# FFN products of blocks 2 on by seven quarter products in place of eight

## The reference, cut to what matters

```python
x = x + layernorm(attn(layernorm(x), wq, wk, wv, wo))   # 16 heads of 64, window 256
h = layernorm(x)
real = h @ cos(theta + theta_noise)                     # [.., 1024] @ [1024, 1024]
imag = h @ sin(phi + phi_noise)
x = x + layernorm(sqrt(real * real + imag * imag))
```

## Time and profile before

| | us |
|---|---|
| median of 3 runs | 2647.22 |
| profiled execution | 2645.41 |
| its span (slowest core) | 2643.8 |
| TensorE busy | 2593.6 |
| VectorE busy | 1252.0 |
| ScalarE busy | 890.6 |
| GpSimd busy | 522.3 |

### The profile page before, as it was taken

One profiled execution on the slowest core, in us unless ns is written; L12 is line 12 of the kernel. 1 busy time (PEld: TensorE's weight loads), 2 busy tenths in 40 slices (PEclk: granted clock), 3 DMA queues, 4 the chain that ended last, 5 costly groups with the idle time before them and its releaser, 6 DMA issues.

```text
span 2643.8 us, 46661 instructions; the slowest of 8 cores (2638.6 to 2643.8 us)
## 1 busy us (share of the span) xinstructions
PE 2593.6 (98%) x17088; PEld 1566.2 (59%) x17088; DVE 1252.0 (47%) x2564; ACT 890.6 (34%) x2061; POOL 522.3 (20%) x676
## 2 busy tenths in 40 slices
PE   7899999999999999999999999999999999999998
PEld 6566575757576666657575666667544444444443
DVE  5445454545454544445454444444463444344442
ACT  4334352525252433424232333333252222222221
POOL 0112132222222221222222121212231101011010
PEclk9999999999999999999999999999999999999999
DMA  7101212212212122220102020110513343333431
GB/s 258 65 18 71 57 64 57 73 41 73 53 61 65 49 65 64 77 60 25 41 25 65 1 65 11 54 33 33 168 58 106 85 120 87 113 99 93 120 83 53
DMA packets 173777, 185.68 MB, mean 70 GB/s; under 512 B 131824, under 2 KB 132080, under 8 KB 173040
## 3 DMA queue, kind: packets, MB, share of 16 engines
q1 hardware_dynamic: 173552, 182.69, 23.5%
HBM read 109.25 MB, written 41.94 MB: 57 GB/s over the span
## 4 chain that ended last, share of the span: by engine, by line
PE 91%; DVE 2%; DMA 2%; ACT 2%; issue 2%; SPq 0%; DVEq 0%; POOL 0%; ACTq 0%; POOLq 0%
PE pb L662 25%; PE pb L289 21%; PE pb L364 13%; PE pb L330 13%; PE pb L429 7%; PE pb L506 6%; PE pb L470 5%; PE pb L564 2%; DMA r_sb<-phb 1%; DMA r_sb<-thb 1%; DVE stats L446 1%; DVE pb L444 0%; SPq L59 0%; ACT p_sb L449 0%; DVE o_sb L611 0%
## 5 line engine op out<-in xcount | busy, mean ns | idle before, releaser
L289 PE MATMUL pb<-xth,wreg 128*128 128x256 bf16 x3840 | 694.0, 273 | 0.0
L458 POOL TENSOR_SCALAR p_sb<-p_sb,stats 128x384 f32<-128x384 f32 (+2 forms) x512 | 345.6, 687 | 1286.1 <-DVE stats L454 614.4
L449 ACT ACTIVATE p_sb<-pb,stats 128x384 f32<-128x384 f32 (+2 forms) x512 | 287.4, 562 | 754.7 <-DVE stats L446 725.7
L289 PE MATMUL pb<-xtl,wreg 128*128 128x256 bf16 x1920 | 523.8, 273 | 0.0
L289 PEld LDWEIGHTS pb<-xth,wreg 128*128 128x128 bf16 x3840 | 375.4, 98 | 109.5 <-issue 64.9
L444 DVE TENSOR_TENSOR pb<-pb,mask_s 128x256 f32<-128x256 f32 (+1 forms) x512 | 210.1, 410 | 324.2 <-PE pb L429 324.1
L662 PE MATMUL pb<-wreg,q_sb 128*128 128x512 bf16 x1536 | 333.0, 379 | 0.0
L364 PE MATMUL pb<-wreg,aoh 128*128 128x512 bf16 x1024 | 309.7, 379 | 0.0
L330 PE MATMUL pb<-wreg,xth 128*128 128x512 bf16 x1024 | 306.2, 381 | 2.3 <-DVE v_sb L342 1.4
L662 PE MATMUL pb<-wreg,xth 128*128 128x512 bf16 x1024 | 306.0, 379 | 0.0
L446 DVE TENSOR_REDUCE stats<-pb 128x1 f32<-128x384 f32 (+2 forms) x512 | 272.8, 533 | 54.2 <-DVE pb L444 1.8
(11 more groups left out here) (63 smaller groups left out, 2408.2 us busy)
## 6 DMA issues: line engine op xcount, KB each, us to landing
x_sb<-x SPq DMA_DIRECT2D x64, 512.0 KB, 4.4
r_sb<-x SPq DMA_DIRECT2D x32, 512.0 KB, 4.7
x<-r_sb SPq DMA_DIRECT2D x32, 512.0 KB, 2.6
wreg<-x SPq DMA_DIRECT2D x32, 512.0 KB, 6.8
y<-wreg SPq DMA_DIRECT2D x64, 256.0 KB, 2.3
trig<-o_sb SPq DMA_DIRECT2D x32, 256.0 KB, 2.8
wreg<-trig SPq DMA_DIRECT2D x4, 2048.0 KB, 18.9
wreg<-wkT SPq DMA_DIRECT2D x4, 1024.0 KB, 14.6
```

Of the source, the lines that this page charges most:

```text
L289: e.matmul(bank[b][:, 0:256], a, r, start=s, stop=z)
L449: texp = ac.inc(lambda e, e2=e2, pu=pu, sc=sc: e.activation(pu, sc, AF.Exp, bias=stats[:, col + e2:col + e2 + 1], scale=1.0, accum_out=sta ...
L458: tok["p", e2, qs] = po.inc(lambda e, e2=e2, pu=pu: e.tensor_scalar(pu, pu, stats[:, col + 4 + e2:col + 5 + e2], 1.0, op0=ALU.mult, op1=AL ...
```

## The change

From block 2 on, the product of a block's rows with a matrix is made of seven products of quarters in place of eight (Strassen's scheme in Winograd's form). A is the block's 256 x 1024 rows, cut into 128 x 512 quarters; B the matrix, cut into 512 x 512 quarters. Four sums of quarters of A are made in float32 on VectorE for each block, four of B (T1 to T4) once. Sums and quarters are then split into high and low parts as before. A product is 4 chunks of K x 3 matmuls of 512 columns. Some products go on in a bank that holds an earlier one; such a bank is first copied (`keep`) or totalled with a kept one (`total`).

The sums of B are made with the chunks: a chunk is now 256 columns out of each half of the columns, of the two 128-row chunks kc and kc+4. There are 16 chunks as before, with 11 parts in place of 7; one in each of groups 1 to 14, two in groups 7 and 14, queued at the end of s=1 in place of s=2. The sums go to a new DRAM tensor, 8 MB of high and low parts in all, and are loaded at the end of the attention stage into wreg[3], k_sb and v_sb. All eight banks serve the FFN from block 2 on, LayerNorm parts stay in `later`, and one part of `later` and one of the next rows' is popped after each product.

```diff
-            which, kc = i // KC, i % KC
+            which, kc, c0 = i // 8, i % 8 // 2, i % 2 * 256
             a, b = r_sb[:, 0:1024], r_sb[:, 1024:2048]
-            return [lambda: trig_load(which, kc, a, b), lambda: None, lambda: None,
+            return [lambda: trig_load(which, kc, c0, a, b), lambda: None, lambda: None,
                     lambda: trig_sum(which, a, b), lambda: trig_sin(which, a, b),
-                    lambda: trig_high(b), lambda: trig_low(which, kc, b)]
+                    lambda: (trig_high(b), quarter_sums(a, b, 0)),
+                    lambda: (trig_low(b), trig_store(which, kc, c0), quarter_sums(a, b, 1)),
+                    lambda: quarter_sums(a, b, 2), lambda: None,
+                    lambda: trig_high(a), lambda: (trig_low(a), sums_store(which, kc, c0))]
...
+        def trig_load(which, kc, c0, a, b):
             sp.wait(tok.get("x2"), tok.get("trig_free"), tok.get("wo_stage"))
             for n, dst in enumerate((a, b)):
-                tok["trig_in"] = sp.dma(c_tl, dst, tr_d[which][n][kc * 128:(kc + 1) * 128, :])
+                for i in range(2):
+                    r0 = (kc + 4 * i) * 128
+                    src = tr_d[which][n][r0:r0 + 128, :].rearrange("p (j c) -> p j c", j=2)[:, :, c0:c0 + 256]
+                    tok["trig_in"] = sp.dma(
+                        c_tl, dst[:, i * 512:(i + 1) * 512].rearrange("p (j c) -> p j c", j=2), src)
...
+        def quarter_sums(a, b, n):
+            q = lambda v, i, w=1: v[:, i * 256:(i + w) * 256]
+            dv.wait(tok["trig_sin"], tok.get("quarters"))
...
+        def trig_high(v):
+            ac.wait(tok["trig_sin"], tok.get("quarters"), tok.get("o_free"), tok.get("trig_st"))
+            tok["trig_hi"] = ac.inc(lambda e: e.activation(obf[:, 0:1024], v, AF.Copy))
...
+        def rows_parts(b):
...
+            def sums12():
+                t = diff(s1, a21, a22, ALU.add, st["xn", 1], *tok["s_rows"])
+                st["s", 0] = diff(s2, s1, a11, ALU.subtract, t)
+
+            def sums34():
+                diff(s3, a11, a21, ALU.subtract, st["xn", 0])
+                st["s", 1] = diff(s4, a12, s2, ALU.subtract, st["s", 0])
...
+            def turn_a():
+                sp.wait(tok["wino", b % 2], st["h", "a"], st["l", "a"], st["h", "a2"], st["l", "a2"])
+                for n, (c, w) in enumerate(((0, 1024), (1024, 512))):
+                    for dst, src in ((dah, xnh), (dal, alo)):
+                        tok["aw", n] = sp.turn(
+                            c_xw[n], dst[:, c:c + w].rearrange("p (k t) -> p k t", t=128), src[:, c:c + w])
...
+            return [lambda: stat(0), lambda: stat(1), rstd, lambda: app(0),
+                    lambda: (app(1), high_a()), lambda: (sums12(), high_a2()),
+                    lambda: (sums34(), high_s(0)), lambda: (low_a(), high_s(1)),
+                    lambda: (low_a2(), turn_a()), lambda: (low_s(0), turn_s(0)),
+                    lambda: (low_s(1), turn_s(1), ends())]
...
+            def p6(r):
+                pe.wait(st["p1", r])
+                t = product(r, "a", ("s", 1), ("t", T2))
+                st["u2", r] = keep(r, "a", 2 + r, t)
...
+            return [lambda f=f, r=r: f(r) for f in (p1, p2, p6, p7, p5, p4, p3) for r in range(2)]
...
-                if s == 2 and g > 0:
-                    for i in range((g - 1) * tpp, min(g * tpp, 2 * KC)):
+                if s == 1 and g > 0:
+                    for i in range((g - 1) * 16 // (NB - 2), min(g * 16 // (NB - 2), 16)):
                         later += trig_chunk(i)
...
+        load_sums(0, [tok["o_pe", NB - 1]])
...
+        turn["banks"] = tuple(range(8))
+        for b in range(2, NB):
+            load_resid2(b)
+            rows = rows_parts(b + 1) if b + 1 < NB else []
+            for n, f in enumerate(wino(b)):
+                f()
+                if later:
+                    later.pop(0)()
+                if n > 0:
+                    run(rows, 1)
```

More of the change, by code:

```diff
@@ L92, in build_nc @@
     trig_d = nc.dram_tensor("trig", [2, 2, 128, KC * D], BF16).ap()
+    sums_d = nc.dram_tensor("sums", [2, 2, 128, 8192], BF16).ap()
     with contextlib.ExitStack() as ctx:
@@ L132, in build_nc @@
         c_y = [new(f"d_y{i}") for i in range(2)]
+        c_ws = [new(f"d_ws{i}") for i in range(2)]
+        c_xw = [new(f"d_xw{i}") for i in range(4)]
         tok = {}
@@ L615, in trig_low, with trig_store @@
+        def trig_store(which, kc, c0):
+            sp.wait(tok["trig_hi"], tok["trig_lo"])
             for n in range(2):
-                tok["trig_st"] = sp.dma(c_ts, trig_d[which, n, :, kc * D:(kc + 1) * D],
-                                        obf[:, n * 1024:(n + 1) * 1024])
+                for i in range(2):
+                    o = (kc + 4 * i) * D
+                    dst = trig_d[which, n, :, o:o + D].rearrange("p (j c) -> p j c", j=2)[:, :, c0:c0 + 256]
+                    src = obf[:, n * 1024 + i * 512:n * 1024 + (i + 1) * 512].rearrange("p (j c) -> p j c", j=2)
+                    tok["trig_st"] = sp.dma(c_ts, dst, src)
+            tok["o_free"] = tok["trig_st"]
@@ L618, in trig_low, with sums_store @@
+        def sums_store(which, kc, c0):
+            tok["trig_free"] = tok["trig_lo"]
+            sp.wait(tok["trig_hi"], tok["trig_lo"])
+            for n in range(2):
+                dst = sums_d[which, n].rearrange("p (q k) -> p q k", q=4)[:, :, kc * 512 + c0:kc * 512 + c0 + 256]
+                src = obf[:, n * 1024:(n + 1) * 1024].rearrange("p (q c) -> p q c", q=4)
+                tok["trig_st"] = sp.dma(c_ts, dst, src)
             tok["o_free"] = tok["trig_st"]
@@ L726, in ffn, with load_sums @@
             return out
+        pbf, ptbf, wbf = p_sb[:].bitcast(BF16), pt_sb[:].bitcast(BF16), wreg[3][:]
+        qrt = [((pbf[:, 0:1536], pbf[:, 1536:3072]), (aoh[:], aol[:])),
+               ((ptbf[:, 0:1536], ptbf[:, 1536:3072]), (xth[:], xtl[:]))]
+        sums = [(wbf[:, 0:8192], wbf[:, 8192:16384]), (k_sb[:].bitcast(BF16), v_sb[:].bitcast(BF16))]
+        hold = [q_sb[:, i * 512:(i + 1) * 512] for i in range(4)]
+        T1, T3, T2, T4 = range(4)
+        def load_sums(r, waits):
+            sp.wait(*waits)
+            for n in range(2):
+                tok["ws", r] = sp.dma(c_ws[r], sums[r][n], sums_d[r, n])
@@ new lines, in wino, with product, keep, part @@
+        def wino(b):
+            par = b % 2
+            bk, st = {}, {}
+            def product(r, name, xp, wp):
+                first = (r, name) not in bk
+                if first:
+                    bk[r, name] = dense_bank()
+                    pe.wait(*bfree[bk[r, name]])
+                bank_ = bank[bk[r, name]]
+                kind, p = xp
+                xh, xl = qrt[par][kind == "s"]
+                pe.wait(tok["wx", par, kind, p], tok["wt", r])
+                if wp[0] == "t":
+                    pe.wait(tok["ws", r])
+                t = None
+                for kc in range(4):
+                    c = p * 512 + kc * 128
+                    if wp[0] == "t":
+                        o = wp[1] * 2048 + kc * 512
+                        ws_h, ws_l = (v[:, o:o + 512] for v in sums[r])
+                    else:
+                        ws_h, ws_l = (f(r, kc + 4 * wp[1], wp[2] * 512, 512) for f in (wh, wl))
+                    for i, (a, w) in enumerate(three(xh[:, c:c + 128], xl[:, c:c + 128], ws_h, ws_l)):
+                        f = lambda e, a=a, w=w, s=(first and kc == 0 and i == 0), z=(kc == 3 and i == 2): \
+                            e.matmul(bank_[:], a, w, start=s, stop=z, skip_group_check=not first)
+                        if kc == 3 and i == 2:
+                            t = pe.inc(f)
+                        else:
+                            pe.do(f)
+                return t
+            def keep(r, name, n, t):
+                ac.wait(t, tok.get(("hold", n)))
+                src, dst = bank[bk[r, name]], hold[n]
+                te = ac.inc(lambda e: e.activation(dst, src[:], AF.Copy))
+                st["keep", n] = te
+                return te
+            def part(r, tt, nh):
+                o = tt * 1024 + nh * 512
+                return (sq, mg)[r][:, o:o + 512]
+            def square(r, tt, nh, src, t):
+                dst = part(r, tt, nh)
+                ac.wait(t, tok.get(("mg", tt, nh)))
+                te = ac.inc(lambda e: e.activation(dst, src, AF.Square))
+                if r == 1:
+                    later.extend(ln_m(b, tt, nh, nh != tt, dst, part(0, tt, nh), te))
+                return te
+            def total(r, name, n, tt, nh, t):
+                dst, src = part(r, tt, nh), bank[bk[r, name]]
+                dv.wait(t, st["keep", n], tok.get(("mg", tt, nh)))
+                te = dv.inc(lambda e: e.tensor_tensor(dst, src[:], hold[n], ALU.add))
+                tok["hold", n] = te
+                square(r, tt, nh, dst, te)
+                return te
+            def p1(r):
+                t = product(r, "a", ("a", 0), ("b", 0, 0))
```

(40 more changed lines are left out.)

93 lines of the change are left out of this document (75 added, 18 removed).

## The result

The changed kernel takes 2682.62 us (median), the kernel before 2647.52: ratio 1.0127, 95% interval 1.0096 to 1.0157. It is slower by some 33 us, where 2657, some 10 us, was forecast. Its profiled execution took 2678.75 us. Runs in which a die was disturbed are left out of the ratio, but are part of the medians that are given.

The account below looks back on a forecast made before the run. TensorE was taken to bound both the FFN and attention stages. The terms -72.5 (FFN), +1 (end), -11.5 (old chunks), +82.6 (first-chunk stall) and +10 (second chunks) sum to +9.6 on 2647.2: 2657 us, range 2618 to 2690.

Parts of the forecast that it names:

- FFN, -72.5: FFN blocks: 168 matmuls in place of 192, 5.18 us less in each of 14 blocks, if TensorE stays the bound.
- FFN blocks don't keep TensorE fed: Rival, FFN blocks: transposes or VectorE come 1.5 us late in each, 21 us more, 2678 us; chance 0.10.
- End, +1: Last block: its last LayerNorm stands on VectorE behind the other rows' apply; between 0 and 2.6 us, taken as +1.
- Stall of the first chunk: Attention groups 1 to 14: VectorE waits 5.5 us at the sum for its load, delaying masks, exponential and TensorE; +82.6 us.
- I take +6.2: First chunk's loads in an attention group: all landed 6.2 us after the first issue at 355.31, so at 361.5.
- the bound of 363: First chunk's loads: latest landing time allowed, 363 us on the trace, giving +7.0 us a group.
- The 5.9 a group: Each of 14 attention groups: +5.5 us from the stall and +0.4 from the clock, +82.6 us in all.
- The sine in front of the copy, +1.7: Attention, s=3: sine ahead of ScalarE's copy makes the attend matmul wait a second time, 1.7 us.
- The clock, +0.4: Attention groups: TensorE at half clock after its 3.8 us wait, mostly covered by the second wait; +0.4 us a group.
- the clock falls in full: Rival, attention groups: slower work uncovered, 14 x 7.2 = 101 us, flush at 14; +32, 2679 us; chance 0.18.
- Second chunks, +10: Groups 7 and 14: four parts flushed at the end of s=5 wait for stores; 5 us each, +10 us.
- Trigonometric work of before, -11.5: Attention groups 1 to 8: the 16 old chunks cost 8 x 1.44 = 11.5 us, which the change takes away.

Follow-up runs that it names:

- one slot later: Changed kernel with one more empty part between a chunk's load and sum, so the sum is at s=3 slot 1: 2608.64 us, ratio 0.9825.

## Why the prediction was right, and where its sizes were off

The direction and the chain were right; the time lies 26 us above the forecast of 2657, near the rival of 2679 and inside the range. Most of that is the two cores on which the loads land late, which the prediction did not think of: on the other six the changed kernel's spans are 2659.3 to 2664.2 us, where 2657 means a span of about 2655 (1.8 less, as for the kernel before).

- **What bounds it:** right. TensorE does not wait in the FFN blocks, and what it waits in the attention stage is lost.
- **FFN, -72.5:** 14 x (41.41 - 36.26) = -72.1. VectorE took 307.52/12 = 25.6 us a block (26.7 forecast), ScalarE 14.1 (14.4). No matmul waited for a transpose. The rival "FFN blocks don't keep TensorE fed" falls: the run with the new FFN alone keeps the whole gain.
- **End, +1:** end of the span less the FFN's part, -70.6 + 72.1 = +1.5.
- **Stall of the first chunk:** the mechanism and its place were right, shown by moving the chunks alone (130.03 to 122.50 us a group). Its size was too small: the new chunks cost 106.6 + 11.5 = 118.1 us in all, where I had 82.6 + 10 = 92.6. The term that was mis-sized is "I take +6.2": 8.7 us in the first six groups on the slowest core, so that the bound of 363, 7.7 us behind the issue, was too low as well. It was not the price of the issues: "about 0.9 of more issue" is near the 0.8 us by which six of the cores differ from the runs of two transfers, and they land at 6.3 to 6.7. The term took one landing for all cores, while the slowest one decides.
- **The 5.9 a group:** on those six cores a group is 5.8 to 6.4 us over 121.77, in the forecast's "127 to 128" or just above. The first wait is right (3.9 us, mean of groups 1 to 7 on core 4, for 3.8). The two terms behind it, 1.7 + 0.4 = 2.1, were 1.98 in group 3 of core 4, though as slower work and not as a wait.
- **The sine in front of the copy, +1.7:** not there on any core: TensorE's waits for that copy at attend are 1.3 us in all at most (200 to 1900 us). TensorE at half clock comes to attend after the copy, or nearly. At full clock there would have been one: an estimate for group 3 is 501.91 + 2.28 = 504.19, 1.4 us before the copy's end at 505.60. Moving the sine alone changed nothing in groups 1 to 6, since the slower work stays.
- **The clock, +0.4:** 1.96 us in group 3 (1.98 on core 4). So the two did overlap, as the prediction had it, but the other way round: the slower work covers the wait. The rival "the clock falls in full" had the size (1.7), and with 2679 the time; that its time fits is luck, for it reached 7.2 a group with a landing of 6.2 and the sine's wait, neither of which is so on the slowest core. The clock's part is read from the windows; no run took it away alone. The Trainium skill ("TensorE: Matmul & The Clock Gate", section "HAM oscillation — how this bites in real kernels") describes a slow start behind each wait for a DMA. These windows agree, 0.50 over 502 to 506, though here TensorE's wait was for an exponential that a DMA held up.
- **Second chunks, +10:** the last group of two is 4.3 us longer than one of one chunk (134.33 to 130.03); group 7 takes 133.71 us, 8.8 more than the 124.9 that it would take with one chunk (118.0 before, less 1.44, plus 8.3): 13 in all. The wait for the stores is there as described (5.04 us), and taking the flush away, and spreading its parts, won back 20 us against the run that queues at s=2, where more parts are left for it.
- **Trigonometric work of before, -11.5:** not measured by itself; in the run with the new FFN alone the old chunks take 123.7 us a group, near the 123.21.

The groups of the second sequence are less long (128.4 us mean of groups 9 to 13); VectorE waits there 5.9 us at the sum against 7.9 in the first. The loads are those of the other matrix, but that is not the reason: cores 2 to 7 are alike in both sequences, and in the run with the new chunks alone cores 4 and 5 are late with both matrices. It is the late pair that was late no longer. Why stays open.

## What to carry to other kernels

A DMA that waits for a buffer starts when the buffer is free, not where it stands in the list; moving its consumer forward by three slots then turns idle time of the queue into a wait on an in-order engine. Before adding work to a hand-made order, look which instruction stands behind each new wait and who needs it: here 7.7 us of waiting on VectorE, otherwise half idle, cost 7.5 us a group. And where the slowest core counts, read the other cores too: the price of a load was 6.5 us on six of them and 8.6 on two. And count the parts against the slots: what is flushed in a bunch waits for itself.

## What the runs showed of the hardware that was not expected

- Four strided loads in a row took SP 0.63 us each, two took 0.38 and 0.50 with the same pieces, two whole-row ones 0.33 and 0.42. From first issue to sum, 1 MB each time, there were 6.55 us for four (the six cores that were not late) and 5.8 for two, with pieces of 4 KB or 1 KB alike (means of groups 1 to 6).
- With four transfers, the two cores of a pair (0 and 1, 2 and 3, and so on) could be late together through a whole sequence, 8.0 to 8.8 us from issue to sum in place of 6.3 to 7.3 (means of groups 1 to 6): cores 0 and 1 of the changed kernel, 6 and 7 one slot later, three pairs with the new chunks alone. With two transfers no core's mean was above 6.2.
- A TensorE wait of 6.15 us was followed by some 4 us of work at half clock (501.91 to about 506), which made 2.28 us of matmuls take 4.24; one of 4.08 us on core 4 did the same (4.26).
